# A selective scan rebuilt as one block, half behind half, with every third product given to GpSimd

## The reference, cut to what matters

```
xn = layernorm(x) * gamma + beta
dt = softplus(xn @ W_dt.T + b_dt)                  # (B, L, 128)
A  = -exp(A_log)                                   # (128, 16)
B_in, C_in = xn @ W_B.T, xn @ W_C.T                # (B, L, 16)
A_bar = exp(dt[..., None] * A)
Bx    = dt[..., None] * B_in[:, :, None, :] * xn[..., None]
h_t = A_bar_t * h_(t-1) + Bx_t                     # for each feature and state
y_t = sum over states of C_t * h_t, plus D_param * x
```

## Time and profile before

| | |
|---|---|
| median of 3 runs | 1778.8 us (1778.77 to 1778.92) |
| the profiled execution | 1779.27 us, of which its span is 1777.5 us |
| TensorE matmuls busy | 1499.6 us, 84% of the span |
| VectorE busy | 1063.5 us, 60% |
| ScalarE busy | 646.7 us, 36% |
| GpSimd busy | 217.7 us, 12% |
| granted TensorE clock, mean | 0.899 |

### The profile page before, as it was taken

The page is one execution under the profiler, slowest core; times in us unless marked ns, Lnnn a source line. Parts: engine busy times, 40 slices in busy tenths (PEclk is TensorE's granted clock), DMA queues, the critical chain, the costliest instruction groups (busy, mean ns, idle before and its releaser), DMA issues. The chain is left out here.

```text
span 1777.5 us, 22019 instructions
## 1 busy us (share of the span) xinstructions
PE 1499.6 (84%) x8172; PEld 686.7 (39%) x8172; DVE 1063.5 (60%) x2616; ACT 646.7 (36%) x936; POOL 217.7 (12%) x231
## 2 busy tenths in 40 slices
PE   2997889985777999998979998988988589996985
PEld 2232344431233344445433333354436323344353
DVE  6796454458946777754454972556455647755354
ACT  3465432224325033333424663422221245552431
POOL 3000010000000533331000000000000103331000
PEclk9898789998969999998987998998996679997788
DMA  5000000020000100000020000000010000000000
GB/s 207 1 1 1 1 1 0 1 104 35 1 0 1 48 1 1 1 1 1 1 78 26 1 1 1 1 1 1 0 72 1 1 1 1 1 1 1 1 1 12
DMA packets 4075, 27.16 MB, mean 15 GB/s; under 512 B 384, under 2 KB 2432, under 8 KB 2944
## 3 DMA queue, kind: packets, MB, share of 16 engines
q1 hardware_dynamic: 2912, 25.22, 3.6%
q10 hardware_dynamic: 1056, 0.52, 0.1%
HBM read 25.21 MB, written 0.52 MB: 14 GB/s over the span
## 5 line engine op out<-in xcount | busy, mean ns | idle before, releaser
L811 DVE TENSOR_REDUCE maxima<-banks 128x1 f32<-128x512 f32 (+4 forms) x640 | 363.1, 604 | 111.0 <-PE banks L660 104.3
L955 ACT ACTIVATE big<-banks 128x1024 f32<-128x1024 f32 (+2 forms) x320 | 294.3, 960 | 265.5 <-PE banks L703 94.2
L688 PE MATMUL banks<-big 32*128 32x512 f32 (+6 forms) x1280 | 232.6, 613 | 17.2 <-DVE big L832 12.9
L660 PE MATMUL banks<-big 32*128 32x77 bf16 (+6 forms) x1024 | 158.3, 297 | 23.5 <-ACT big L238 6.1
L1476 DVE TENSOR_TENSOR big<-big,banks 128x512 f32<-128x512 f32 (+1 forms) x116 | 79.7, 687 | 152.6 <-PE banks L1389 147.2
L724 PE MATMUL banks<-big,v_heads 128*9 128x512 f32 (+7 forms) x1024 | 159.6, 569 | 6.3 <-ACT heads_out L871 3.2
L477 POOL TENSOR_TENSOR rstd<-mean_var,minus_half 128x4 f32<-128x4 f32 x34 | 34.9, 1026 | 1033.9 <-DVE mean_var L399 1033.9
L1451 ACT ACTIVATE big<-banks 128x512 f32<-128x512 f32 (+1 forms) x116 | 69.1, 596 | 179.1 <-PE banks L1388 179.0
L660 PEld LDWEIGHTS banks<-big 32*128 32x128 bf16 (+1 forms) x1024 | 57.3, 97 | 182.0 <-DVE maxima L811 93.5
L1419 PE MATMUL banks<-big,moe_weights 128*128 128x512 f32 (+1 forms) x232 | 119.8, 601 | 3.0 <-ACT big L1459 2.6
L688 PEld LDWEIGHTS banks<-big 32*128 32x128 f32 (+3 forms) x1280 | 72.8, 178 | 70.3 <-ACT big L955 23.7
(11 more groups left out here) (410 smaller groups left out, 2216.5 us busy)
## 6 DMA issues: line engine op xcount, KB each, us to landing
moe_weights<-in_moe SPq DMA_DIRECT2D x1, 4864.0 KB, 14.5
moe_weights<-in_moe SPq DMA_DIRECT2D x1, 4768.0 KB, 22.5
moe_weights<-in_moe SPq DMA_DIRECT2D x1, 3264.0 KB, 10.5
moe_weights<-in_l3x SPq DMA_DIRECT2D x1, 3072.0 KB, 9.6
late_weights<-in_l2x SPq DMA_DIRECT2D x1, 2048.0 KB, 8.8
moe_weights<-in_l SPq DMA_DIRECT2D x1, 1234.0 KB, 13.1
rows<-in_rows SPq DMA_DIRECT2D x1, 1152.0 KB, 8.1
late_weights<-in_turned SPq DMA_DIRECT2D x1, 1152.0 KB, 16.9
```

The source lines that it names most:

```text
L660: last = nc.tensor.matmul(RING[n % NR][:, x * klen:x * klen + last_key(t)], q[rows, t * P:(t + 1) * P], ks[rows, 0:last_key(t)], start=Tru ...
L688: last = nc.tensor.matmul(SC[pair % 2][0:size, j % 2, n0:S], ks[rows, i * P:i * P + size], q[rows, n0:S], start=True, stop=turned)
L811: nc.vector.tensor_reduce(dst, src, AX_X, ALU.max).then_inc(ring_free.up(), 1)
L955: nc.scalar.activation(E[pair % NEP][0:size, :, n0:S], SC[pair % 2][0:size, :, n0:S], ACT.Exp, scale=scale).then_inc(exp_ready.up(), 1)
```

## The change

- The four blocks become one. Softplus is made half by half, with the minimum and the maximum read straight from the PSUM banks. `D * x` is added by TensorE, as products of the tiles of `XT` with a diagonal matrix.
- The rows of B and C stay float32: B's 16 rows start at partition 0, C's at partition 32. Their copying to all partitions is two float32 products with 32 rows each, from two different groups of partitions.
- The order is half 0's 16 states, then half 1's. There are two pairs of input banks in place of three, since the sums and the norm need banks too.
- `ch` is added up tile by tile, with `ch` as the weights and the identity as the moving operand, so that the sum comes out in natural layout. The turning back (L335) falls away.
- The norm of half 0 is put into the loop of half 1: sum and statistics behind step 17, the power by GpSimd, normalising behind step 19, turning behind step 21, moving behind step 23. Half 1's dt is finished behind step 2 (`time_steps(1)`).
- In steps 1, 4, 7, 10, 13, 16, 19, 22, 25 and 28 the product `ch` is GpSimd's, from C rows that ScalarE copies from PSUM into SBUF first (`c_rows`).

The core of the diff:

```diff
+    own = Norms(c, None, [Norm(c.X, turned=[(c.XT, None, None)])], c.X, sums=(6, 7), turned=(4, 5, 0, 1))
+    steps = [(n, z) for z in range(2) for n in range(N)]
+    by_pool = [s % 3 == 1 and n < N - 1 for s, (n, _) in enumerate(steps)]
+    def tile_products(z, src, right, start, stop):
+        for k in range(ST):
+            last = nc.tensor.matmul(c.bank[own.SUM[z]][:, k * P:(k + 1) * P], src[:, k * P:(k + 1) * P], right, ...)
         @block.tensor
             def inputs(s):
-                if s >= 3:
-                    pe.wait_ge(ch_ready.sem, ch_ready.at(s - 2))
-                nc.tensor.matmul(BC[2 * (s % 3)][:, :], pick[:, n, :], x, start=True, stop=True)
-                nc.tensor.matmul(BC[2 * (s % 3) + 1][:, :], pick[:, N + n, :], x, ...).then_inc(in_ready.up(), 1)
+                if s >= 2 and by_pool[s - 2]:
+                    pe.wait_ge(driven.sem, driven.at(s - 1))
+                    pe.wait_ge(c_moved.sem, c_moved.at(pool_steps(s - 2)))
+                elif s >= 2:
+                    pe.wait_ge(ch_ready.sem, ch_ready.at(dve_steps(s - 2)))
+                for j in range(2):
+                    rows = slice(32 * j, 32 * j + 32)
+                    last = nc.tensor.matmul(c.bank[2 * (s % 2) + j][:, :], pick[rows, n, :], bc[rows, zs[z]], ...)
+                last.then_inc(in_ready.up(), 1)
             for s, (n, z) in enumerate(steps):
-                if s + 2 < len(steps):
-                    inputs(s + 2)
-                pe.wait_ge(ch_ready.sem, ch_ready.at(s + 1))
-                nc.tensor.matmul(YS[z][:, :], c.ident[:], ch[:, s % 2, :], ...).then_inc(sum_ready.up(), 1)
+                if not by_pool[s]:
+                    await_product(pe, s)
+                if s < LAST - 1:
+                    inputs(s + 2)
+                if by_pool[s]:
+                    await_product(pe, s)
+                tile_products(z, ch[:, s % 2, :], c.ident[:], False, n == N - 1).then_inc(done.up(), 1)
         @block.scalar
+                scalar.activation(a[:, s % 2, :], dtT[:, zs[z]], ACT.Exp, ...).then_inc(a_ready.up(), 1)
+                if by_pool[s]:
+                    act.wait_ge(in_ready.sem, in_ready.at(s + 1))
+                    scalar.copy(c_rows, c.bank[2 * (s % 2) + 1][:, :]).then_inc(c_moved.up(), 1)
         @block.vector
+            def time_steps(z):
+                dve.wait_ge(soft_ready.sem, soft_ready.at(z + 1))
+                seq(dve, step, vector.tensor_tensor(dtT[:, zs[z]], mx[:, zs[z]], ex[:, zs[z]], ALU.add))
+                seq(dve, step, vector.tensor_tensor(uT[:, zs[z]], dtT[:, zs[z]], xnT[:, zs[z]], ALU.mult))
+                vector.tensor_copy(c.small[:, z:z + 1], ...).then_inc(dt_ready.up(), 1)
+                vector.tensor_tensor_scan(h[:, s % 2, :], a[:, s % 2, :], bx[:, s % 2, :], ...).then_inc(decay_used.up(), 1)
                 drive(s + 1)
+                if not by_pool[s]:
+                    vector.tensor_tensor(ch[:, s % 2, :], h[:, s % 2, :], c.bank[2 * (s % 2) + 1][:, :], ...)
+                if s == 2:
+                    time_steps(1)
+                if s == 17:
+                    own.own_sum(dve, 0)
+                    own.own_stats(dve, 0, 0)
+                if s == 19:
+                    own.own_norm(dve, 0, 0)
         @block.gpsimd
+                if by_pool[s]:
+                    pool.wait_ge(c_moved.sem, c_moved.at(pool_steps(s)))
+                    pool.wait_ge(decay_used.sem, decay_used.at(s + 1))
+                    await_summed(pool, s - 2)
+                    nc.gpsimd.tensor_tensor(ch[:, s % 2, :], h[:, s % 2, :], c_rows, ALU.mult).then_inc(ch_pool.up(), 1)
-    norms(c, turned_back(c, yT), [Norm(c.X, turned=[(c.XT, None, None)])], c.X)
```

More of the change, by code:

```diff
@@ L358, in pe_rest @@
         for pair in range(NT // 2 if final.turned else 0):
[L359 to L362, removed]
+            self.turn_pair(pe, pair)
         for half in range(2 if final.plain_turned is not None else 0):
@@ L463, in dve_rest @@
         if final.turned:
[L464 to L466 removed]
+            self.move_pair(dve, vector, 3)
         if final.plain_turned is not None:
@@ L498, in act_rest @@
         for pair in range(3 if final.turned else 0):
[L499 to L505, removed]
+            self.move_pair(act, scalar, pair)
         if final.plain_turned is not None:
@@ L1595, in layer1_scan @@
     ex, mx = c.big1(3 * TOK, TOK), c.big1(4 * TOK, TOK)
[L1598 to L1601, removed]
+    bc = c.big1(5 * TOK, TOK)[0:64]
+    weights, diag = c.big1(6 * TOK, 64), c.big1(6 * TOK + 64, P)
+    pick = c.big3(0, N * P)[0:64].rearrange("p (n m) -> p n m", n=N)
@@ L1602, in layer1_scan @@
     a, bx, h, ch = (c.big3(2048 + 1024 * i, TOK).rearrange("p (z t) -> p z t", z=2) for i in range(4))
[L1603 to L1649, removed]
-            nc.gpsimd.tensor_copy(weights[:, :, N:2 * N], c.m("L1_WCT").unsqueeze(1).broadcast_to([P, 3, N])).then_inc(weights_ready.up(), 1)
-            nc.gpsimd.tensor_copy(pick[:, 0:N // 2, :], c.pick_id[:, 0:N // 2].unsqueeze(2).broadcast_to([96, N // 2, P]))
@@ new lines, in await_product @@
+    def await_product(eng, s):
+        if by_pool[s]:
+            eng.wait_ge(ch_pool.sem, ch_pool.at(pool_steps(s)))
+        else:
+            eng.wait_ge(ch_ready.sem, ch_ready.at(dve_steps(s)))
+    def tile_products(z, src, right, start, stop):
+        for k in range(ST):
+            last = nc.tensor.matmul(c.bank[own.SUM[z]][:, k * P:(k + 1) * P], src[:, k * P:(k + 1) * P], right, start=start and k == 0,
+                                    stop=stop and k == ST - 1, skip_group_check=True)
+        return last
@@ new lines, in inputs @@
+                for j in range(2):
+                    rows = slice(32 * j, 32 * j + 32)
+                    last = nc.tensor.matmul(c.bank[2 * (s % 2) + j][:, :], pick[rows, n, :], bc[rows, zs[z]], start=True, stop=True)
+                last.then_inc(in_ready.up(), 1)
+            for z in range(2):
+                nc.tensor.matmul(c.bank[z][:, :], c.m("L1_WdtT"), xnT[:, zs[z]], start=True, stop=True).then_inc(dt_made.up(), 1)
+            pe.wait_ge(weights_ready.sem, weights_ready.at(1))
@@ L1676, in _ @@
+                done = own.sum_ready if n == N - 1 else summed
+                tile_products(z, ch[:, s % 2, :], c.ident[:], False, n == N - 1).then_inc(done.up(), 1)
+                if s == 21:
+                    own.turn_pair(pe, 0)
+                    own.turn_pair(pe, 1)
+            own.turn_pair(pe, 2)
+            own.turn_pair(pe, 3)
         @block.scalar
         def _(act):
+            scalar.activation(c.negA, c.m("L1_A_log"), ACT.Exp).then_inc(neg_ready.up(), 1)
+            for z in range(2):
+                act.wait_ge(abs_ready.sem, abs_ready.at(z + 1))
+                last = scalar.activation(ex[:, zs[z]], ex[:, zs[z]], ACT.Exp)
@@ L1683, in _ @@
+            own.move_pair(act, scalar, 2)
         @block.vector
```

138 lines of the change are left out of this document (108 added, 30 removed).

## The result

The changed kernel takes 1810.7 us (median of 6 runs, 1804.5 to 1817.2), the kernel before 1779.1 us in the same comparison (6 runs, 1778.8 to 1780.4). The ratio is 1.0181, 95% interval 1.0155 to 1.0207. The forecast was 1776.0 us within 1770.5 to 1783.

The account below looks back on a forecast made before the run. VectorE was taken to bound the scan loop. Head -7.9, tail -5.0, work in the loop +4.85, steps +2.7 and clock +2.5 sum to -2.85, so 1778.8 became 1776.0 us, range 1770.5 to 1783.

Parts of the forecast that it names:

- the clock: Start of the scan loop: TensorE at half clock for some 10 us from 413 on, +2.5 us.
- The rival of the clock: Scan loop: TensorE becomes the bound, 1.5 us per further half-clock step; with five steps 1783.7 us; chance 0.14.
- Head: Before the loop: first scan at about 412.05 instead of 419.99, -7.9 us.
- Tail: Behind the last `ch`: 6.9 us in place of 11.9, -5.0 us.
- Work in the loop: Scan loop, VectorE: `time_steps(1)`, half 0's sum and statistics, and its norm, +4.85 us.
- this rival: Scan loop: the work put in is free because VectorE waits for inputs anyway; at most 1 us, no chance of its own.
- The scan standing still beside GpSimd: Scan behind a GpSimd step: waits out GpSimd's product and ends 1.08 us behind it; likeliest case, 0.50.
- The rival without it: Scan loop: the scan doesn't stand still beside GpSimd, 2.7 us less, 1773.3 us; chance 0.28.
- The inputs' delay: Scan loop: input products reach `drive` 0.17 us late, twice in three steps; part of the +2.7 us for steps.
- The two input products side by side: Scan loop, TensorE: both take 0.96 to the next product, 1.14 to their end; rival one behind the other, 1790 us, 0.05.

Follow-up runs that it names:

- e2: Changed kernel plus two more 32-row input products per step on rows 64 to 127, up to step 20; 1790.3 us, ratio 1.0058.
- e5: Changed kernel plus two more 32-row products per step on rows 0 to 63, already in use, up to step 20; 1844.8 us, ratio 1.0373.
- e9: Kernel before with only the float32 inputs, two products of 32 rows, four blocks and three bank pairs kept; 1828.7 us, ratio 1.0269.
- e7: Changed kernel with the inputs again two bfloat16 products of 96 rows, GpSimd's steps kept; 1771.6 us, ratio 0.9975.
- e8: Changed kernel with bfloat16 inputs of 96 rows and no GpSimd steps, VectorE making all products; 1776.1 us, ratio 0.9976.
- e1: Changed kernel plus five float32 products of 512 columns keeping TensorE busy ahead of the loop; 1814.3 us, ratio 1.0195.
- e6: Changed kernel plus four float32 products of 512 columns on all 128 rows at step 3 alone; 1790.7 us, ratio 1.0087.

## Why the prediction was wrong

**The step that failed** is the clock: "I expect half clock again, for some 10 us from 413 on as before from 418", priced at +2.5. It began about where it was put, at 411.9, and lasted 92.2 us in place of some 10. The 22 steps from the scan at 417.85 to the one at 506.53 took 88.7 us; at the forecast's 2.4 us a step and with its 4.85 us of work put into the loop they would have taken 57.7. So the low clock cost 31 us where +2.5 stood. The rival of the clock named this price per step, 1.5 us, but got a chance of 0.14 and was worked out for five steps. The argument against it, "TensorE is busier now", was the error: it took busy time for what the clock follows. Before, the clock had come up in a loop of products with 96 and 128 rows; I carried that over to products with 32 rows in two groups, 64 rows at work of 128. For their time I took L688, where all four groups are at work, and didn't ask whether their clock would be the same. e2 and e5 show that it isn't, e9 that this alone suffices.

The Trainium skill ("TensorE: Matmul & The Clock Gate", Part 1) states that a busy TensorE is released to 2.4 GHz and an idle one held at 1.2. Here it was busy for 82.00 of 82 us, and for 122.00 of 122 in e9, and held at 1.2; the measurement decides.

**The other steps**, by their own numbers:

- Head: forecast -7.9, measured -7.5 (412.46). The first product ended later (the clock was 0.50 up to 405.1), so VectorE began at 402.55, 1.1 us after the 401.47 of the forecast; the wait for ScalarE took up part of that. The table load came ahead of its wait, at 410.34, and not behind it; the first decay was ready about 0.4 us later than forecast all the same.
- Tail: -5.0, measured -5.0 (6.9 us).
- Work in the loop: steps 3 and 18 came 6.0 and 6.6 us behind the ones before them (scans at 417.85 and 423.90, 478.06 and 484.70), and the steps behind them 2.5 and 2.3, so at 4.0 us a step most of it was hidden, where +4.85 was put. The forecast had called this rival worth 1 us at most.
- The scan standing still beside GpSimd: right. 1.59 us, and 1.87 in e7, each ended 1.08 behind GpSimd, as L1613 did. The rival without it is out. The Trainium skill's rule on the shared read interface ("SBUF — State Buffer", Who interferes with whom) agrees with these scans.
- The inputs' delay: 0.27 us in place of 0.17 a time. TensorE started the 32-row products 0.14 us behind the end of `ch` (506.62 to 506.76), not 0.05. Three steps took 7.39 in place of 7.2 at full clock; over ten times that would be 1.9 us (an estimate), but only the last eight steps ran so.
- The two input products side by side: right, 1.13 us from start to end.

With 31 in place of 2.5 the same sum is -2.85 - 2.5 + 31 = +25.7, against 27.3 measured at the stage's end; the head (0.4) and the inputs of the last steps (0.6) make up most of the rest. The remaining 6 us of the span come from the clock in unchanged stages, as shown above. How the scan's timing reaches there isn't settled. Nor is the spread: 13 us among the 6 runs of the changed kernel against 1.6 among those of the kernel before, whose 23 runs beside e5 to e8 spread over 9.8.

## What to carry to other kernels

Before you trade a wide product for one with few rows, look at how many of the 128 rows are at work at once, not only at how long it takes: here the 32-row form took about the time that was planned at full clock, but didn't bring a low clock back. In a trace, a low granted clock over a stretch where TensorE is always busy is the sign; filling the idle row groups, with the same work on rows already in use as the control, shows whether that is the cause, and a short dense piece of 128-row work brought the clock back here. Look, too, for single waits of TensorE in the loop, since one stood before each of the four falls in e1, e2 and e6. And price a clock rival by the whole loop, not by the stretch that the old kernel happened to have.

## What the runs showed of the hardware

- The granted clock stayed at 0.50 for 75 to 122 us with TensorE recorded busy all the time, with two groups of 32 rows alternating with 128-row products, and stood at 1.00 over 34 us with four groups in the same places (TensorE busy 28.53 of 34). Once up, it stood at 1.00 for 40.9 us with two groups as well (e6).
- Four falls from 1.00 within a loop (e1, e2 twice, e6) came 1.2 to 1.7 us after a wait of TensorE of 1.6 to 2.3 us; waits of 0.38 to 0.44 us in two of three steps had not brought it down over 38 us (e6).
- At 1.2 GHz four products of 128 columns with a weight load each take the same 2.0 us as one of 512 columns.
- At 2.4 GHz four float32 products in four groups of 32 rows took 1.08 us, two took 1.06.
- A TENSOR_TENSOR_SCAN that meets a running GpSimd product ends 1.08 us behind it, in 1.35 us (e1) to 2.04 (e7) as they overlap less or more, against 1.22 alone.
